# First batch of an adaLN block: normalised and turned before wmod is known, then scaled by feature tile

## The reference, cut to what is computed

```
mod = (silu(c) @ wmod).reshape(2, 6, 1, 1024)       # sa, ca, ga, sb, cb, gb per batch
ga, gb = sign(.) * max(|.|, 0.25)
h = layernorm(x) * (1 + ca) + sa                    # x: 2 x 1024 x 1024, float32
q, k, v = h @ wq, h @ wk, h @ wv                    # 32 heads of 32, rotary on q and k
x = x + ga * (softmax(causal(q k^T / sqrt(32))) v @ wo)
h = layernorm(x) * (1 + cb) + sb
x = x + gb * (h @ W_base^T + b_base + mixture of 8 low-rank experts)
```

## Time and profile before

| | us |
|---|---|
| median of 3 runs | 1825.47 (1824.23 to 1825.47) |
| profiled execution | 1819.76 |
| its span | 1818.0 |
| TensorE busy | 1643.7 (90%), granted clock 0.945 on average |
| VectorE, ScalarE, GpSimd busy | 1010.9, 985.4, 611.1 |

### The profile page before, as it was taken

The page is one execution under the profiler, slowest core; times in us unless marked ns, Lnnn a source line. Parts: engine busy times, 40 slices in busy tenths (PEclk is TensorE's granted clock), DMA queues, the critical chain, the costliest instruction groups (busy, mean ns, idle before and its releaser), DMA issues.

```text
span 1818.0 us, 29711 instructions
## 1 busy us (share of the span) xinstructions
PE 1643.7 (90%) x9459; PEld 1196.8 (66%) x9459; DVE 1010.9 (56%) x3248; ACT 985.4 (54%) x2368; POOL 611.1 (34%) x483
## 2 busy tenths in 40 slices
PE   3667989999999998899999999999879999999997
PEld 0235666666666765677667667666457888888885
DVE  1535547667576664556666666665535445445443
ACT  1333667887887776667777777777742101101110
POOL 1441424334343230423433332331322333333342
PEclk8788999999999998999999999998589999999998
DMA  9633233444443338223323323223443211211210
GB/s 338 226 135 76 74 86 91 108 122 109 129 114 77 97 77 247 57 61 96 72 68 97 71 68 97 67 60 78 119 132 93 70 59 45 70 49 56 69 48 34
DMA packets 170786, 174.52 MB, mean 96 GB/s; under 512 B 20898, under 2 KB 120562, under 8 KB 170644
## 3 DMA queue, kind: packets, MB, share of 16 engines
q1 hardware_dynamic: 166484, 164.42, 32.5%
q10 hardware_dynamic: 4160, 8.39, 1.4%
HBM read 96.68 MB, written 25.21 MB: 67 GB/s over the span
## 4 chain that ended last, share of the span: by engine, by line
PE 63%; ACT 10%; DVE 10%; issue 8%; DMA 4%; POOL 3%; SPq 2%; ACTq 0%; DVEq 0%; POOLq 0%
PE ps_s L1186 12%; PE ps_s L661 10%; PE ps_qkv L1186 9%; PE ps_pv L1254 7%; PE ps_s L1229 7%; PE ps_t L1197 6%; ACT rows_sb L1436 4%; PE ps_s L622 3%; PE ps_s L623 3%; PE ps_s L624 3%; DVE rows_sb L1657 2%; ACT probsT L1472 1%; DVE bias_m L1675 1%; PE ps_qkv L663 1%; DVE ps_s L1698 1%
## 5 line engine op out<-in xcount | busy, mean ns | idle before, releaser
L1436 ACT ACTIVATE rows_sb<-rows_sb,bias_m 128x640 f32<-128x640 f32 (+7 forms) x512 | 398.1, 778 | 228.1 <-DVE bias_m L1675 227.8
L1657 DVE CUSTOM_DVE_ANT_0 rows_sb<-ps_t,mask 128x512 f32<-128x512 f32 (+3 forms) x512 | 296.8, 586 | 157.6 <-PE ps_t L1197 150.9
L1472 ACT ACTIVATE probsT<-ps_s 128x512 f32<-128x512 f32 (+2 forms) x640 | 321.5, 549 | 13.4 <-PE ps_s L1229 12.5
L1197 PE MATMUL ps_t<-stk 96*128 96x512 f32 (+3 forms) x768 | 277.5, 366 | 45.5 <-DVE m_rows L1688 25.7
L1229 PE MATMUL ps_s<-stk 98*128 98x512 f32 (+3 forms) x768 | 238.7, 392 | 16.2 <-DMA stk<-m_rows 12.0
L1698 DVE TENSOR_TENSOR ps_s<-ps_s,mask_t 128x128 f32<-128x128 f32 (+1 forms) x384 | 121.4, 340 | 184.5 <-PE ps_s L1229 182.8
L1197 PEld LDWEIGHTS ps_t<-stk 96*128 96x128 f32 x768 | 151.8, 198 | 102.8 <-DVE m_rows L1688 36.7
L1229 PEld LDWEIGHTS ps_s<-stk 98*128 98x128 f32 x768 | 135.9, 199 | 107.6 <-issue 51.9
L1254 PE MATMUL ps_pv<-probsT,v_all 128*32 128x256 f32 (+1 forms) x2816 | 189.3, 363 | 1.3 <-ACT probsT L1472 1.3
L1822 POOL TENSOR_TENSOR rope_b<-rope_b,rope_sin 128x512 f32<-128x512 f32 x64 | 82.2, 1284 | 278.0 <-DVE rope_b L1642 278.0
L1657 DVE CUSTOM_DVE_ANT_0 rows_sb<-ps_t,mask,smax_part 128x128 f32<-128x128 f32 (+3 forms) x256 | 140.8, 550 | 49.8 <-PE ps_t L1197 23.5
(11 more groups left out here) (190 smaller groups left out, 3085.9 us busy)
## 6 DMA issues: line engine op xcount, KB each, us to landing
stk<-rot SPq DMA_DIRECT2D x384, 128.0 KB, 2.4
probsT<-in_L_wmod_dram SPq DMA_DIRECT2D x5, 2048.0 KB, 8.3
wm_one<-in_L_wmod_dram SPq DMA_DIRECT2D x5, 2048.0 KB, 9.0
w_raw<-in_L_attn_wq_dram SPq DMA_DIRECT2D x16, 512.0 KB, 4.0
w_raw<-in_L_attn_wk_dram SPq DMA_DIRECT2D x16, 512.0 KB, 4.4
w_raw<-in_L_attn_wv_dram SPq DMA_DIRECT2D x16, 512.0 KB, 4.1
attn_scratch<-attn_sb SPq DMA_DIRECT2D x128, 64.0 KB, 3.1
a_raw<-attn_scratch SPq DMA_DIRECT2D x16, 512.0 KB, 4.9
```

The lines of the kernel that those rows point to most:

```text
L1197: pe.matmul(bank[:, 0:c1 - c0], stk[0:3 * HD, u % 2, 0, qt // 4, h, qt % 4 * P:(qt % 4 + 1) * P], stk[0:3 * HD, u % 2, 1, part, h, 0:c1 - ...
L1436: act.activation(row, row, ACT.Exp, bias=bias_m[:, qt, h:h + 1], scale=SCALE, accum_out=sums[:, qt // 4, h, qt % 4:qt % 4 + 1]).then_inc(s ...
L1472: act.activation(probsT[:, w % 4, hs[0]:hs[-1] + 1, 0:n], s_bank[(NS * u + k) % 3][:, 0:len(hs) * n].rearrange("p (h n) -> p h n", h=len(hs)),
L1657: dve.tensor_tensor_reduce(rows_sb[:, to, at + c0:at + c1], bank[:, 0:n], mask[:, BANK - n:BANK] if last else mask[:, 0:1].broadcast_to([P ...
```

## The change

The eight token tiles of batch 0 are normalised and transposed while the first four wmod chunks are loaded, two tiles ahead of each chunk in the queue and on TensorE. They go unscaled into `xT` (`ln_out`, a copy on VectorE and one on ScalarE per tile); `x_start` has four buffers for that, and the transposes four PSUM banks. The partial sums of a chunk are summed to columns (`mod_cols`: four products with 2 columns each, the partial sums as weights), which VectorE takes from PSUM as `shift_a` and `scale_a` (`mod_vectors`), with no trip to DRAM. Then each feature tile of 512 tokens is scaled in one VectorE instruction (`ln_mod`), rounded in one (`ln_round`), and its rest is taken by VectorE for even `kt` and by GpSimd for odd (`ln_rest`). A projection waits for each feature tile by itself.

Chunks 4 to 7 stand behind the four projections, chunks 8 to 11 behind rows 1, 4, 7 and 11 (`LATE_MOD`). `first_rows` has 96 products: also `chain(1, 0)` and `chain(1, 1)`, so that stages 0 and 1 have three projections each. The gates are made as columns, turned once and written to `gate_dram`; the scale and shift of the second normalisation (`shift_b`, `scale_b`) stay in SBUF, and their reload after attention is gone.

```diff
-    whole = t == 0 or (t + 1) % G == 0
+    whole = (t + 1) % G == 0
...
+ROPE_AT[0, 0] = ROUND_AT[0, 2] = (1, 1)
...
-FIRST_M0, FIRST_V0 = 13, 16
+FIRST_CHAINS, LEAD = [(0, 4), (0, 5), (1, 0), (1, 1)], 8
+BEHIND = [5] * EARLY_ROWS + [3] * (NR - EARLY_ROWS)
+assert LEAD + sum(BEHIND) == 3 * KT * len(FIRST_CHAINS)
+FIRST_M0, FIRST_V = 13, (5, 10)
+LATE_MOD = {1: 8, 4: 9, 7: 10, 11: 11}
...
+            load_x(0)
+            load_x(1)
             load_wmod(0)
-            load_x(0)
+            load_x(2)
+            load_x(3)
             load_wmod(1)
-            load_x(1)
+            load_x(4)
+            load_x(5)
             load_wmod(2)
+            sp.dma_start(rope_tab, rope_c).then_inc(rope_ld, 16)
+            load_w(0, 0)
+            load_x(6)
+            load_x(7)
             load_wmod(3)
-            load_w(0, 0)
...
-            for k in range(FIRST_MOD):
-                store_mod(k)
...
-            for i in range(NT):
-                if i + 2 < NT:
-                    load_x(i + 2)
-                if i + 6 < MODC:
-                    load_wmod(i + 6)
-                store_mod(i + FIRST_MOD)
+            load_wmod(6)
             load_w(0, 1)
+            load_wmod(7)
+            sp.wait_ge(ln_tr, 2 * NT)
+            stack(0, 0)
+            load_wmod(8)
             load_w(1, 1)
-            sp.wait_ge(mod_st, 16 * MODC)
+            load_wmod(9)
+            stack(0, 1)
+            load_wmod(10)
+            load_wmod(11)
             sp.wait_ge(mod_mm, MODC)
-            for b in range(B):
-                sp.dma_start(mcol_rows[b * 16:(b + 1) * 16, :], mod_dram[b, 3 * D:5 * D].rearrange(
-                    "(r p) -> r p", p=P)).then_inc(mcol2_ld, 16)
+            stack(1, 0)
...
-            sp.wait_ge(ln_hi, 2 * NT)
-            sp.wait_ge(ln_lo, 2 * NT)
-            sp.wait_ge(ln_tr, 2 * NT)
-            for u in range(2):
-                for c in range(2 - u):
-                    stack(u, c)
...
+            sp.wait_ge(gate_ev, 1)
+            sp.dma_start(gate_dram.rearrange("s (k p) -> (s k) p", p=P), gate_rows).then_inc(gate_st, 16)
...
+            def mod_cols(k):
...
-                pe.matmul(ps_pv[0:B, 0:BANK], sel[:, :], mod_part, start=True, stop=True).then_inc(mod_sum, 1)
+                if k % FIRST_MOD == 0 and k:
+                    pe.wait_ge(mcol, k // FIRST_MOD)
+                for j in range(4):
+                    at = (k % FIRST_MOD * 4 + j) * B
+                    mm = pe.matmul(ps_pv[:, at:at + B], mod_part[k % 2][:, j * P:(j + 1) * P], sel[:, :],
+                                   start=True, stop=True)
+                mm.then_inc(mod_sum, 1)
             def ln_half(b, tt, half, bank):
...
+                    if t == 0 and n in (0, 2) and way == 0:
+                        pe.wait_ge(ln_hi, KT * c + kt + 1)
+                        if kt % 2:
+                            pe.wait_ge(ln_lo, KT // 2 * c + kt // 2 + 1)
+                        else:
+                            pe.wait_ge(ln_lo_even, KT // 2 * c + kt // 2 + 1)
...
                 mod_chunk(k)
                 if k:
-                    mod_rows(k - 1)
-            mod_rows(FIRST_MOD - 1)
...
-            for i in range(NT):
-                for half in range(2):
-                    if i:
-                        pe.wait_ge(ln_tt[half], i)
-                    ln_half(0, i, half, ln_bank[half])
-                mod_chunk(FIRST_MOD + i)
-                if i == 0:
-                    pe.wait_ge(mcol, 1)
-                mod_rows(FIRST_MOD + i)
...
-                if 4 <= i < 6:
-                    chain(0, i - 4, 0, 3 * KT)
-            chain(0, 2, 0, 3 * KT)
-            chain(0, 3, 0, 3 * KT)
-            pe.wait_ge(mod_rw, MODC)
+                    mod_cols(k - 1)
+            mod_cols(FIRST_MOD - 1)
+            for n in range(4):
+                chain(0, n, 0, 3 * KT)
+                if n:
+                    mod_cols(FIRST_MOD + n - 1)
+                mod_chunk(FIRST_MOD + n)
             def first_rows():
-                cuts = [LEAD + (6 * KT - LEAD) * k // NR for k in range(NR + 1)]
-                v_products(0, LEAD)
+                m = LEAD
+                products(0, m)
+                mod_cols(2 * FIRST_MOD - 1)
                 for k in range(NR):
                     row(0, k)
-                    v_products(cuts[k], cuts[k + 1])
+                    products(m, m + BEHIND[k])
+                    m += BEHIND[k]
+                    if k - 1 in LATE_MOD:
+                        mod_cols(LATE_MOD[k - 1])
+                    if k in LATE_MOD:
+                        mod_chunk(LATE_MOD[k])
...
+                    if k in FIRST_V:
+                        turn_v(0, FIRST_V.index(k))
+                pe.wait_ge(gate_ok, 1)
+                pe.transpose(ps_pv[0:MODG, 0:P], gate_col, ident[:, :]).then_inc(gate_t, 1)
...
+                for i, (t, c) in enumerate(FIRST_CHAINS):
+                    if m0 < (i + 1) * n and m1 > i * n:
+                        chain(t, c, max(m0 - i * n, 0), min(m1 - i * n, n))
...
             def mod_out(k):
                 act.wait_ge(mod_mm, k + 1)
-                if k:
-                    act.wait_ge(mod_sum, k)
-                act.copy(mod_part, ps_s[0][:, 0:BANK]).then_inc(mod_ev, 1)
...
+                if k >= 2:
+                    act.wait_ge(mod_sum, k - 1)
+                act.copy(mod_part[k % 2], ps_s[0][:, 0:BANK]).then_inc(mod_ev, 1)
+            def ln_out(tt):
...
+                act.copy(xT[:, 4:8, tt * P:(tt + 1) * P],
+                         ln_bank[tt % 2][1].rearrange("p (k t) -> p k t", k=4)).then_inc(ln_tt[1], 1)
...
+                act.wait_ge(h_ok, KT * c + kt + 1)
+                cols = slice(c * BANK, (c + 1) * BANK)
+                act.copy(hT_hi[:, kt, cols], xT[:, kt, cols]).then_inc(ln_hi, 1)
             def next_mod(tt, half):
...
+                ln_out(2 * k + 1)
+                if k == FIRST_MOD - 1:
+                    for q in range(4):
+                        rope_table(q)
+                    for n in range(2):
+                        split_qk(0, n)
                 mod_out(k)
-            for n in range(4):
+            for kt in range(KT):
+                ln_round(0, kt)
+            for n in range(2, 4):
                 split_qk(0, n)
+            mod_out(4)
+            for kt in range(KT):
+                ln_round(1, kt)
+            mod_out(5)
             for half in range(2):
                 split_v(0, half)
-            act.wait_ge(mcol, 1)
-            for i in range(NT):
-                ln_split(i, 0)
-                ln_mod(i, ln_bank[1])
-                ln_split(i, 1)
-                mod_out(FIRST_MOD + i)
-                if 1 <= i < 3:
-                    rope_table(2 * i - 2)
-                    rope_table(2 * i - 1)
...
+                split_qk(1, n)
...
+            row_exps(0, 2)
             copy_vT(0, 0)
+            mod_out(9)
+            row_exps(0, 3)
+            copy_v(0, 0)
+            for n in range(2, 4):
+                split_qk(1, n)
+            row_exps(0, 4)
+            mod_out(10)
+            copy_vT(0, 1)
+            row_exps(0, 5)
+            copy_v(0, 1)
+            mod_out(11)
+            row_exps(0, 6)
+            row_exps(0, 7)
             round_m(0, 0)
-            for i in range(5, 8):
-                row_exps(0, i)
-            copy_v(0, 0)
             for i in range(8, NU):
                 row_exps(0, i)
-            copy_vT(0, 1)
-            copy_v(0, 1)
-            for n in range(4):
...
-                for kt in range(4):
-                    o = dve.tensor_scalar(h_start[:, 0, kt * P:(kt + 1) * P], bank[:, kt * P:(kt + 1) * P],
-                                          modcol1[:, 8 + kt:9 + kt], modcol[:, kt:kt + 1], ALU.mult, ALU.add)
-                o.then_inc(ln_tt[0], 1)
+                dve.tensor_copy(xT[:, 0:4, tt * P:(tt + 1) * P],
+                                ln_bank[tt % 2][0].rearrange("p (k t) -> p k t", k=4)).then_inc(ln_tt[0], 1)
+            def ln_mod(c, kt):
+                if kt == 0:
+                    for half in range(2):
+                        dve.wait_ge(ln_tt[half], 4 * (c + 1))
+                part = xT[:, kt, c * BANK:(c + 1) * BANK]
+                dve.tensor_scalar(part, part, scale_a[:, B * kt:B * kt + 1], shift_a[:, B * kt:B * kt + 1], ALU.mult,
+                                  ALU.add).then_inc(h_ok, 1)
...
+            def ln_rest(c, kt):
+                dve.wait_ge(ln_hi, KT * c + kt + 1)
+                cols = slice(c * BANK, (c + 1) * BANK)
+                dve.tensor_tensor(hT_lo[:, kt, cols], xT[:, kt, cols], hT_hi[:, kt, cols].bitcast(F32),
+                                  ALU.subtract).then_inc(ln_lo_even, 1)
...
-            for k in range(FIRST_MOD):
-                mod_store(k)
...
             for i in range(NT):
-                if i + 1 < NT:
-                    ln_stats(0, i + 1)
-                ln_mod(i, ln_bank[0])
```

(49 more changed lines are left out.)

234 lines of the change are left out of this document (104 added, 130 removed).

## The result

| | before | after |
|---|---|---|
| median | 1824.85 (1820.2 to 1825.47, 4 runs) | 1764.39 (1761.33 to 1767.88, 4 runs) |
| profiled execution, span | 1819.76, 1818.0 | 1762.54, 1760.4 |
| E | 177.94 | 140.91 |
| first row exponential of u=1 | 190.43 | 150.32 |
| M | 276.22 | 220.14 |

The ratio is 0.9675, with a 95% interval of 0.9648 to 0.9701. The forecast was 1775 in 1758 to 1794. The kernel is faster, as forecast, by 60.5 us of medians where 50.7 had been worked out. Ratios leave out one run of the kernel before, of 2255.7 us at a granted clock of 0.64, where all its others had 0.93 to 0.95.

What follows compares the result with a forecast made beforehand. The start was taken to be bound by hand-offs. Scale known at 51, first rows done at 144, plus 81.5 to u=3's first exponential at 225.5: 50.7 us earlier, so a median of 1775, range 1758 to 1794.

Steps and rivals of the forecast that it cites:

- E: End of the last row maximum of stage u=0, rows scored before TensorE's main loop; forecast 144, 34 us earlier.
- M: First 128x128 row exponential of stage u=3; forecast 225.5, 50.7 us earlier, with that shift carried to the end.
- Part 1, T0: Start until the scale is known: tile 7 and chunk 3 near 40, then TensorE's queue; 51, between 47 and 54.
- Part 2, scaling: Scaling by feature tile with four projections: VectorE and GpSimd in turn, 3.2 us a pair, 13 us for 512 tokens.
- The first rival, free engines: Scaling: GpSimd and VectorE overlap, projection 0 ends at 58.5, end at 1763 to 1766; chance 0.14.
- Part 3, first rows: First score rows with 96 products: 42 us of TensorE after 96.7, plus 2 for chunk 8, 1 gates, 2 clock.
- The wait above chunk 8: First rows: TensorE waits about 2 us for wmod chunk 8's landing and not for any later chunk.
- Part 4, E to M: Stages u=0 and u=1: 11 us to the first exponential of u=1, then 70.5; 81.5 in all, before 98.3.
- no m_rows stall over 1 us: Stages u=0 and u=1: sign that the earlier 4.64 us stall on m_rows is gone.
- One of its own signs of being wrong: First stage: the prediction is wrong if its rows wait for the rope ring rather than for TensorE.
- The rival that the moved projections save nothing: Stages u=0 and u=1 keep their length less the stall, end 1785; 0.18 shared with late chunks, beyond 1788.
- The rival of the clock: Start: thin chunks and short waits lower TensorE's clock, slower if 51 of 75 us run at half speed; chance 0.04.

Runs made afterwards that it cites:

- trip: The changed kernel with the attention norm's scale and shift columns sent through DRAM and back before scaling; median 1768.1 us, ratio 0.9708.
- rope_early: The changed kernel with TensorE's sixteen rope turns and ScalarE's copies moved ahead of the turn of x tile 6; median 1756.9 us, ratio 0.9657.
- w8_first: The changed kernel with the load of wmod chunk 8 issued ahead of the stacking of the first rotated tiles; median 1758.5 us, ratio 0.9661.
- no_moved: The changed kernel with projections 0 and 1 of the second head group back in stages u=0 and u=1; median 1775.2 us, ratio 0.9738.
- whole_wait: The changed kernel with projections 0 and 2 waiting for all eight feature tiles of their tokens; median 1765.0 us, ratio 0.9720.
- combo3: The changed kernel with chunk 8 first, early rope turns, all subtractions on VectorE, splits between rotations, second group's rotations later; median 1742.3 us, ratio 0.9600.
- all_dve: The changed kernel with all sixteen subtractions on VectorE, none on GpSimd; median 1758.2 us, ratio 0.9659.

## Why the prediction was right, and where its sum was off

**The size of the miss.** The prediction turned 1819.8 into 1769.1 for a profiled execution; 1762.54 was measured, 6.6 less. The other 4.0 to the median came from the step that added 5.7 because the median of before lay that far above its profiled execution. The median of after lies 1.9 above its own. That offset is scatter and should not have been carried.

**Part 1, T0.** 51 forecast, 50.25 measured, by the mechanism named: tile 7 reaches TensorE at 40.78 (40 forecast), and turns (some at the lower level), chunk 3 and sums follow. The 51 was a choice between 47 and 54, so its closeness to 50.25 is in part luck: seven profiles range over 1.3 us. trip and rope_early show it from both sides.

**Part 2, scaling.** Right in kind, 2.81 instead of 3.2 us a pair. The terms were 0.82 for two scalings, 0.69, 1.26 and 0.45 for hand-offs. The rows show 1.00, 0.69, 0.97 (what GpSimd's 1.27 costs VectorE) and 0.15: the hand-offs were the step that was too dear. Projection 0 ended at 62.75 (65), projection 3 at 89.9 (93.8), the rings at 82.8, 89.0, 96.2 and 102.3 (87, 93, 100, 106). The first rival, free engines, needed 1.00 for every two scalings and falls with the 1.97. The end alone would have spoken for it: its 1763 to 1766 holds the measured 1764.4, which the forecast of 1775 misses by 10.6. Only the rows tell them apart (projection 0 at 62.75 against its 58.5, E at 140.91 against its 136).

**Part 3, first rows.** The start was 4 earlier, the wait for chunk 8 was 3.10 (2 forecast) and its sixteen products ran at the lower level (3.64), and E came 3.1 earlier (140.91 for 144). The wait above chunk 8 that the prediction excluded did not appear in the kernel after. It stands close behind: w8_first met it at chunk 10.

**Part 4, E to M.** 79.2 measured, 81.5 forecast: 9.4 to the first exponential of u=1 (11), 69.8 for the two stages (70.5). The prediction's mark was that no m_rows stall over 1 us would be left. The DMA stall of 4.64 is gone, but another stands there: TensorE waits 2.57 us for VectorE's m_rows at 150.53, behind the rotation at the head of VectorE's queue. The prediction saw that ring on ScalarE and not on VectorE. One of its own signs of being wrong, rows of the first stage that wait for the rope ring, is thereby met in one place; the total came out shorter all the same, since the other terms were too long. The rival that the moved projections save nothing is refuted by no_moved; but they saved 9.7 of the 16 that the stages alone show.

**After M.** The end gained 1.1 more than M did (57.2 and 56.1). Of the 28 distances between first exponentials after M, 15 are the same to 0.1; the others are up to 2.6 shorter and up to 2.0 longer, so this sign of the prediction did not hold. In sum they are 3.2 shorter (1003.3 for 1006.5), and what follows them is 1.8 longer. The repeat of the same kernel has 1007.2 for that sum, and the two largest shortenings, 2.6 and 2.1, are 0.5 and 0.0 there: at least these are scatter. Others come back in the repeat (+1.5, +1.8, -1.9); with one profile of the kernel before, whether they belong to the change stays open.

**The rival of the clock.** TensorE's granted clock rose with the change (0.92 for 0.87 in 97 to 181), where the rival of a lower clock wanted half speed for 51 of 75 us. The prediction held 0.2% (3.7 us) to be enough to tell from no change; eleven runs of the kernel before on one chip range from 1812.5 to 1830.4, so for a single run that is too fine.

## What to carry to other kernels

Where a start is a string of hand-offs, mark three or four points that every variant has, and measure each edit between them: edits of 1 to 4 us are plain there and lost in the medians. Work moved out of a full stage is paid for where it lands, and most of the price was not its own time but what it made an in-order engine wait for at the head of its queue; look there first, and expect a wait that is taken out of one slot to turn up a few slots later. Before giving a second engine half of a job, see whether its instruction slows the first: here one engine alone did the whole job faster.

## What the runs showed of the hardware

**The end scatters by more than the edits, and the clock does part of it.** A line through the mean times of the thirteen rows of the table over their M has a slope of 1.00 (give or take 0.08), with a standard deviation of 2.0 us around it (whole_wait lies 4 below). So a shift at M reaches the end one for one, and one such set of runs is good to some 2 us. One place where it scatters is the passage from the last stages to the next phase. The stretch from 1230 to 1290 in the kernel after, in combo3 and in whole_wait:

```profile
1230.00:1290.00 60.00, 44.90 (x233) 24.20 (x233) 19.00 (x63) 36.74 (x72) 21.23 (x9) 0.57 0.43 110
```

```profile
1230.00:1290.00 60.00, 42.09 (x282) 28.06 (x283) 21.12 (x49) 29.63 (x59) 16.41 (x9) 0.86 0.54 147
```

```profile
1230.00:1290.00 60.00, 41.85 (x255) 22.36 (x255) 24.32 (x83) 41.09 (x87) 21.23 (x9) 0.70 0.39 102
```

The granted clock is 0.57, 0.86 and 0.70 there, and the time from the last first-row exponential to the end of the span is 537.0, 531.4 and 531.1 us, though nothing of that part differs between the three programs. The stretch falls on slightly different work in each. Taken from that exponential on, the next 70 us have 0.59, 0.77 and 0.75, and over the fourteen profiles, before included, the time to the end falls as this clock rises (correlation -0.76). This is shown as going together, not as a cause; what sets the clock there was not tested.

**A product of 2 columns costs as much as one of 128.** In all_dve a column sum takes 0.95 us at the higher level, recorded as eight operations of 2 columns with 128x128 weights. Eight transposes with 128 columns take 1.07 in rope_early:

```profile
67.19 0.95 PE L1129 MATMUL ps_pv<-sel,x_next 128*128 128x2 f32 x8
```

From start to start the eight operations stand 0.11 us apart, and so do the transposes; the 0.95 and 1.07 differ by the first and the last operation. A sixty-fourth of the columns saves nearly nothing. That the load of the 128x128 weights sets this pace is likely, since both have it, but was not tested. The bound of 0.6 for a sum, which the prediction named and did not take, is not reached.
